# Earlier rows, an earlier tail for the next-to-last batch, and q stacked by PE for two batches

## What is computed

```python
x = x + jnp.tanh(g_xattn[0]) * _L0_xattn_ref(_layernorm(x, axis=-1), ctx_1024, ...)
x = x + jnp.tanh(g_ffn[0]) * _L0_ffn_ref(_layernorm(x, axis=-1), ...)
x = x + jnp.tanh(g_xattn[1]) * _L1_xattn_ref(_layernorm(x, axis=-1), ctx_1024, ctx_1024, mask, ...)
x = x + jnp.tanh(g_ffn[1]) * _L1_ffn_ref(_layernorm(x, axis=-1), ...)
```

## Time and profile before

| | |
|---|---|
| Three runs | 451.64, 458.64, 460.27 us |
| The profiled execution | 455.05 us, of which the span is 453.3 us |
| PE busy | 339.5 us (75% of the span) |
| PE weight loads | 249.3 us (55%) |
| DVE busy | 253.6 us (56%) |
| ACT busy | 156.5 us (35%) |
| POOL busy | 149.8 us (33%) |
| TensorE's granted clock, mean | 0.855 of 2.4 GHz |

### The profile page before, as it was taken

How to read it: one execution, slowest core, us unless ns; L and a number is a source line. 1 busy time by engine, 2 the same in 40 slices (tenths; PEclk the granted TensorE clock), 3 DMA queues, 4 the chain that set the end, 5 groups by cost and what they waited for, 6 DMA issues and landing times. The chain is left out here.

```text
span 453.3 us, 6857 instructions
## 1 busy us (share of the span) xinstructions
PE 339.5 (75%) x2066; PEld 249.3 (55%) x2066; DVE 253.6 (56%) x846; ACT 156.5 (35%) x370; POOL 149.8 (33%) x172
## 2 busy tenths in 40 slices
PE   2468979888969776466887999997577719988870
PEld 2236545545435665465664575653277609878770
DVE  2759565666365566136747677865463604535542
ACT  2312344434322253124222455362221305444440
POOL 3211211215040340431062102274536565645560
PEclk9867699998695899569869999999787867999995
DMA  7436987940044283776440231013565366869934
GB/s 268 128 75 158 300 230 220 290 133 17 2 148 136 78 246 101 242 219 164 106 129 6 62 80 48 14 35 91 196 199 168 119 172 191 284 187 324 371 139 139
DMA packets 67908, 70.42 MB, mean 155 GB/s; under 512 B 7933, under 2 KB 50691, under 8 KB 67872
## 3 DMA queue, kind: packets, MB, share of 16 engines
q1 hardware_dynamic: 41904, 52.24, 39.6%
q10 hardware_dynamic: 22448, 11.41, 8.7%
q0 software_dynamic: 3520, 6.34, 4.3%
HBM read 40.66 MB, written 21.81 MB: 138 GB/s over the span
## 5 line engine op out<-in xcount | busy, mean ns | idle before, releaser
L963 PE MATMUL ps_s<-xT,fw 128*128 128x128 f32 x488 | 77.7, 303 | 17.0 <-DVE xT L1301 8.6
L963 PEld LDWEIGHTS ps_s<-xT,fw 128*128 128x128 f32 x488 | 69.4, 215 | 20.1 <-DVE xT L1301 10.4
L668 ACT ACTIVATE probs<-ps_s 103x512 f32<-103x512 f32 (+1 forms) x96 | 56.2, 596 | 65.4 <-PE ps_s L872 57.8
L1152 DVE TENSOR_REDUCE negm<-ps_a 128x4 f32<-128x308 f32 x128 | 55.1, 470 | 29.5 <-PE ps_a L852 23.1
L574 POOL DMA_INDIRECT routed<-pay,slot x48 | 48.0, 1001 | 57.1 <-DVE slot L1261 45.9
L592 POOL DMA_INDIRECT expert_out<-xt x46 | 45.8, 996 | 35.1 <-ACT xt L733 25.2
L852 PE MATMUL ps_a<-ks,qs 128*128 128x308 f32 x128 | 42.3, 366 | 10.4 <-DVE negm L1152 5.5
L1291 DVE SCALAR_TENSOR_TENSOR qr<-qr,ps_s 128x256 f32<-128x256 f32 x46 | 19.2, 418 | 53.9 <-ACT qr L723 32.6
L871 PE MATMUL ps_s<-qs,ks 128*103 128x512 f32 (+1 forms) x96 | 47.7, 496 | 1.9 <-issue 0.7
L548 POOL TENSOR_SCALAR ve<-mv 128x4 f32<-128x4 f32 x16 | 3.7, 230 | 121.1 <-DVE mv L1102 121.1
L872 PE MATMUL ps_s<-augT,aug 128*103 128x512 f32 (+1 forms) x96 | 40.3, 420 | 0.0
(11 more groups left out here) (156 smaller groups left out, 559.6 us busy)
## 6 DMA issues: line engine op xcount, KB each, us to landing
fw<-f_in SPq DMA_DIRECT2D x46, 384.0 KB
routed<-xt ACTq DMA_DIRECT2D x2, 5568.0 KB, 23.8
fw<-f_in SPq DMA_DIRECT2D x30, 321.0 KB
qs<-qhl SPq DMA_DIRECT2D x128, 64.0 KB, 2.0
xt<-routed SPq DMA_DIRECT2D x46, 65.0 KB
xt<-routed SPq DMA_DIRECT2D x30, 64.0 KB
routed<-xt SPq DMA_DIRECT2D x30, 64.0 KB
routed<-pad SPq DMA_DIRECT2D x18, 65.0 KB, 2.1
```

Of the source, the lines that this page charges most:

```text
L668: nc.scalar.activation(probs[0:KSIZE[j], s, :], ps_s[(NS * n + s) % SCORE_BANKS][0:KSIZE[j], :], ACT.Exp, scale=SCALE).then_inc(exp_ok, 1)
L963: last = nc.tensor.matmul(up_bank[j % 2][:, c * P:(c + 1) * P], weights_of(j)[:, c * P:(c + 1) * P], xT[j % 2][:, :], start=True, stop=True)
L1152: nc.vector.tensor_reduce(negm[:, i, g * HPG:(g + 1) * HPG], a[:, 0:GK].rearrange("p (h k) -> p h k", h=HPG), AX.X, ALU.max, negate=True). ...
```

## The change

**An earlier tail for n = 2 and n = 6.** A new table moves their stages. In steps from the layer's first score tile: normalise2 47 to 44, turn2 47 to 45, router 49 to 46, route_exp 50 to 47, ranks 52 to 48, the four scatters 53, 55, 58, 59 to 49, 49, 50, 50. stats2 stays at 43.

**Earlier rows for parts 1 and 3.** The part's first three row loads are issued five steps before the part instead of all seven one step before; the rest follow one a step.

**An earlier second layer.** `SECOND` goes from 95 to 93, and with it all of that layer's steps. In `RETURNED_FRONT` the results of n = 6 stay at 99, and its high half moves into the step of its projection.

**q of n = 4 and 5 stacked by PE.** For these two batches the 16 DMAs are gone. PE multiplies each half by a selection matrix, two matmuls of 128x512 per group. Even groups go to ps_t and are copied out by ACT, odd groups to the ring and are copied out by DVE. The selection tile grows from 1024 to 1280 columns, so that one tile serves k and q.

```diff
+TAIL_NEXT_TO_LAST = {
+    "stats2": 19, "normalise2": 20, "turn2": 21, "router": 22, "route_exp": 23, "ranks": 24,
+    "scatter0": 25, "scatter1": 25, "scatter2": 26, "scatter3": 26,
+}
-SECOND = 95
+SECOND = 93
 RETURNED_FRONT = [
-    {"gather": 70, "results": 77, "stats": 77, "normalise": 78, "turn": 79, "project": 80, "high": 81, "low": 81, "maxima": 85,
-     "split": 93, "augment": 93},
-    {"gather": 73, "results": 82, "stats": 82, "normalise": 83, "turn": 85, "project": 87, "high": 88, "low": 88},
-    {"gather": 90, "results": 99, "stats": 99, "normalise": 100, "turn": 101, "project": 102, "high": 103, "low": 103},
-    {"gather": 93, "results": 104},
+    {"gather": 70, "results": 77, "stats": 77, "normalise": 78, "turn": 79, "project": 80, "high": 81, "low": 81, "spread": 82, "maxima": 83,
+     "split": 91, "augment": 91},
+    {"gather": 73, "results": 82, "stats": 82, "normalise": 83, "turn": 85, "project": 87, "high": 88, "low": 88, "spread": 90},
+    {"gather": 90, "results": 99, "stats": 99, "normalise": 100, "turn": 101, "project": 102, "high": 102, "low": 102},
+    {"gather": 93, "results": 103},
 ]
+BY_PE = [NB, NB + 1]
...
-                        if k == TILE_AT[p] + max(-1, t - ROWS_AHEAD):
+                        if k == TILE_AT[p] + max(-5 if p % 2 else -1, t - ROWS_AHEAD):
                             load_rows(p, t)
                 for n in due("low", k):
-                    spread_q(n)
+                    if n not in BY_PE:
+                        spread_q(n)
...
+            def take_even(n):
+                act.wait_ge(sc_full, NS * (n - 2))
+                for i, g in enumerate(range(0, GROUPS, 2)):
+                    act.wait_ge(q_turn, 2 * BY_PE.index(n) + i + 1)
+                    nc.scalar.activation(qs[n % 3][:, g, :], ps_t[:, :], ACT.Copy).then_inc(q_even, 1)
...
+            def spread_q(n):
+                pe.wait_ge(qh_ok, n + 1)
+                pe.wait_ge(ql_ok, n + 1)
+                for g in range(GROUPS):
+                    if g % 2 == 0:
+                        turn_bank_free(q_even, 2 * BY_PE.index(n) + g // 2 + 1)
+                    bank = ring() if g % 2 else ps_t
+                    for c in range(2):
+                        last = nc.tensor.matmul(bank[:, :], copies(Q_COPIES, c, g), qhl[c][n % 2][:, :], start=c == 0, stop=c == 1)
+                    last.then_inc(ring_full if g % 2 else q_turn, 1)
...
+            def take_odd(n):
+                dve.wait_ge(sc_full, NS * (n - 2))
+                for g in range(1, GROUPS, 2):
+                    a = ring()
+                    nc.vector.tensor_copy(qs[n % 3][:, g, :], a[:, :]).then_inc(q_odd, 1)
```

More of the change, by code:

```diff
@@ L131, in at_step, with spreads_by_pe @@
         return SECOND_FRONT + AT[stage]
-    return SECOND * l + NS * b + (TAIL[stage] if b == NB - 1 and stage in TAIL else AT[stage])
+    tail = {NB - 1: TAIL, NB - 2: TAIL_NEXT_TO_LAST}.get(b, {})
+    return SECOND * l + NS * b + tail.get(stage, AT[stage])
+def spreads_by_pe(k):
+    return [n for n in BY_PE if at_step(n, "spread") == k]
 def due(stage, k):
@@ L212, in two_layers @@
         cx4 = sb("cx4", [P, NB, HPG, KEYS])
-        select = sb("select", [P, 2, GROUPS, 4, 32], F32R)
+        select = sb("select", [P, GROUPS, 10, 32], F32R)
         maski = sb("maski", [P, TPB, KEYS], I32)
@@ L351, in pay_rows, with by_dma @@
             return slice((n % 2) * TPB, (n % 2 + 1) * TPB)
+        def by_dma(n):
+            return len([m for m in range(n % 3, n + 1, 3) if m not in BY_PE])
         def score_tile(s):
@@ L534, in link @@
                 pool.wait_ge(s_pool, chain.next() + 1)
[L536 removed]
+            nc.gpsimd.memset(select[:, :, :, :].bitcast(F32), 0.0).then_inc(s_select, 1)
             nc.gpsimd.memset(half[:, :], -0.5)
@@ L642, in _ @@
             act.wait_ge(ld_id, 16)
-            for c in range(2):
-                nc.scalar.activation(select[:, c, :, 2 * c:2 * c + 2, :], bcast(ident.rearrange("p (g r) -> p g r", g=GROUPS), 2, 2), ACT.Copy).then_inc(s_select, 1)
+            for pair in (select[:, :, 6:8, :], select[:, :, 1:4:2, :]):
+                nc.scalar.activation(pair, bcast(ident.rearrange("p (g r) -> p g r", g=GROUPS), 2, 2), ACT.Copy).then_inc(s_select, 1)
             def copy_nT(n):
@@ L651, in high_q @@
                 act.wait_ge(q_ok, n + 1)
-                if n >= 2:
+                if n - 2 in BY_PE:
+                    act.wait_ge(q_even, 2 * (BY_PE.index(n - 2) + 1))
+                    act.wait_ge(q_odd, 2 * (BY_PE.index(n - 2) + 1))
+                elif n >= 2:
                     for g in range(GROUPS):
-                        act.wait_ge(qspread[(n - 2) % 3][g], 64 * ((n - 2) // 3 + 1))
+                        act.wait_ge(qspread[(n - 2) % 3][g], 64 * by_dma(n - 2))
                 nc.scalar.activation(qhl[0][n % 2][:, :], qr1[:, :], ACT.Copy).then_inc(qh_ok, 1)
+            def take_even(n):
[3 more added lines that the diff above has]
+                    nc.scalar.activation(qs[n % 3][:, g, :], ps_t[:, :], ACT.Copy).then_inc(q_even, 1)
             def copy_augT(n):
@@ L755, in _ @@
                         nc.scalar.activation(aug[:, :, :].rearrange("p g k -> p (g k)"), augf, ACT.Copy).then_inc(s_aug, 1)
+                for n in spreads_by_pe(k):
+                    take_even(n)
                 for n in due("augment", k):
@@ L788, in ring, with copies @@
                 return ps_a[u % RING]
+            def copies(at, c, g):
+                return select[:, g, at[c]:at[c] + 4, :].rearrange("p b r -> p (b r)")
             def keys(l):
@@ L805, in spread_keys @@
                     for c in range(2):
-                        last = nc.tensor.matmul(bank, select[:, c, g, :, :].rearrange("p c r -> p (c r)"), khl[c][:, :], start=c == 0, stop=c == 1)
+                        last = nc.tensor.matmul(bank, copies(K_COPIES, c, g), khl[c][:, :], start=c == 0, stop=c == 1)
                     last.then_inc(ring_full if l else k_full, 1)
@@ L819, in values, with turn_bank_free @@
                 last.then_inc(ring_full, 1)
-            def transposes(src, done, read, value):
+            def turn_bank_free(read, value):
                 if reader:
@@ L824, in transposes @@
                 reader.append((read, value))
+            def transposes(src, done, read, value):
+                turn_bank_free(read, value)
                 for i in range(TPB):
@@ L844, in scores_for_max @@
                     pe.wait_ge(ks_ok, 2 * (l + 1))
-                if i == 0:
-                    pe.wait_ge(qspread[n % 3][g], 64 * (n // 3 + 1))
+                if i == 0 and n in BY_PE:
+                    pe.wait_ge((q_even, q_odd)[g % 2], 2 * BY_PE.index(n) + g // 2 + 1)
+                elif i == 0:
+                    pe.wait_ge(qspread[n % 3][g], 64 * by_dma(n))
                 bank = ring()
@@ L1147, in low_q @@
                 nc.vector.tensor_tensor(qhl[1][n % 2][:, :], qr1[:, :], qhl[0][n % 2][:, :].bitcast(F32), ALU.subtract).then_inc(ql_ok, 1)
+            def take_odd(n):
[3 more added lines that the diff above has]
+                    nc.vector.tensor_copy(qs[n % 3][:, g, :], a[:, :]).then_inc(q_odd, 1)
+                    dve.wait_ge(q_odd, 2 * BY_PE.index(n) + g // 2 + 1)
+                    dve.sem_inc(ring_used, 1)
             def maxima(n, u):
@@ L1337, in _ @@
                     low_q(n)
+                for n in spreads_by_pe(k):
+                    take_odd(n)
                 for n in due("output", k):
```

2 lines of the change are left out of this document (added).

## The result

The changed kernel takes 463.65 us (median of 4 runs, 463.13 to 468.62) where the kernel before took 455.82 (4 runs, 451.64 to 460.27): a ratio of 1.027, 95% interval 1.017 to 1.037. Two of the four runs of the kernel before, 458.64 and 460.27 us, lie over 1.5% above its fastest and are left out of the ratio, so it stands for 12 us, where the medians differ by 7.8. It is slower, and by more than was forecast: the sum was +9.4 on the profiled execution, and 465 us is 6.4 above the median of 458.64.

The account below looks back on a forecast made before the run. PE, busy 75% of the span, plus its waits was taken as the bound. Terms +7 - 3 + 1.4 + 0.5 + 6.5 - 1 - 2 = +9.4 on 455.05 gave 464.5; 465 us was predicted, range 446 to 472.

Parts of the forecast that it names:

- The first layer's end: End of the first layer's attention: PE's work moved behind pay's wait runs at half clock, ranks waits for choose; +7 us.
- Part 1's rows: Step from part 0 to part 1: PE's idle 7.13 us shrinks, gather starts later, results of n = 4 come sooner; -3 us.
- The front: Second layer's front, 211.00 to 229.80: two steps fewer against q's DVE copies and PE matmuls; +1.4 us, bounds -4 and +5.
- The two steps: Before the second layer's first score tile: two steps fewer, half of 3.2 us taken as gain; -1.6, bounds 0 and -3.2.
- nothing covers the matmuls: Upper bound for the second layer's front, +5 us: q's matmuls on PE find no empty time to cover them.
- n = 6: High half in its projection's step: ACT may wait for DVE's bias, with tiles queued behind it; +0.5 us.
- The second layer's end: PE's 3.03 us move behind pay's wait, ranks waits for choose, part 2's rows' wait is filled; +6.5 us, bounds +5.1 and +8.0.
- Parts 2 and 3: Part 3's row wait of 1.19 us goes, -1 us; scatters of n = 6 issued ahead of part 2's put-outs, -2 us.
- POOL's relief: Part 2: n = 6's eight scatters precede the put-outs, two of them leaving the back-to-back run; -2 us, bounds 0 and -15.
- D: Rival, chance 0.15: SP's row loads delay the last write-back and gather by 4.5 us, n = 4's results follow; 472 us.
- C: Rival, chance 0.18: released clock, and the late waits in 347.50 to 374.40 go, -12 instead of -2; 443.6 us.
- B: Rival, chance 0.22: moved matmuls release the throttled clock, so both layers' ends cost less; about 454 us.

## Why the prediction was right, and where its steps were not

The forecast was 465 us in a range of 446 to 472; 463.65 was measured. That it came so close is in good part luck. The forecast stood on runs of 451.64 to 460.27 us, and the kernel before, run beside the experiments, takes about 452: the change costs 12 us by the ratio and 13.5 in the trace, where +9.4 was summed. And of the seven terms four come out near in this trace, two are too small and one is too large; one of the four, the rows, does so in this trace only.

- **The first layer's end.** Forecast +7, bounds +1.7 and +7.7 (its terms add up to 5.5 + 1.9 = 7.4 at most); the trace has +4.3, the tail of n = 2 alone costs 1.009. The mechanism is as told, with a wait of 6.60 us where some 6.5 was written. The moved work and the wait of ranks came as priced: 5.1 us, where 5.5 was written, and 1.33. What was mis-sized is what followed at half clock before: the router is 0.9 us shorter, weigh2 0.4, and the copies of k and the turns behind it 1.2. The granted clock was 0.50 from 133.37 to 138.5, then full until about 142, 0.50 again through most of weigh2, and full from about 145.6; the kernel before stayed at 0.50 from 135.05 to 146.96. The rule of the Trainium skill, page "TensorE: Matmul & The Clock Gate", section "What's actually happening", by which activity releases the throttle, is borne out here more than the row of before made me grant. It did not hold for long: after ranks' wait of 1.33 us, five small matmuls and the first of two of 308 columns, the half clock was back. At the second layer's end of the changed kernel the router did not get the full clock (1.71 us); with the tail alone it did (1.01).
- **Part 1's rows.** Forecast -3, built of 5 us on PE and a gather 4.5 us later. The trace: -6.0, then +2.9, together -3.1. But the three other traces with the same edit have -0.9, -1.1 and -1.9 over these two stretches, and those without it +0.1 to -2.1, so a gain of 3 us is not there, and the rows alone are worth nothing (1.001). The step that failed is that the results would come with the gather and so 3 us sooner: they do wait for the gather now, and it comes too late to gain. The last write-back is 5.4 us later and the first gather 6.0, of which 2.6 are the first layer's end; from part 0's first tile on they come 2.7 and 3.3 us later, where 4.5 was written.
- **The front.** Forecast +1.4; the trace has +5.4. The two steps show -1.2 alone (forecast -1.6), which is inside the scatter. The step that failed priced q by its copies on DVE, 3.0 us, and let PE's empty 5.2 us cover the matmuls. They don't cover: each of the two trains stands bare on PE for 2.5 us, with DVE waiting for it and copying, 4.4 us in the trace with q alone. The bound of +5 for "nothing covers the matmuls" was the case. The two parts make 3.2 of the 5.4 us; the rest is not assigned.
- **n = 6.** Forecast +0.5 for its halves in one step; the trace has +5.2, and moving its front two steps back is worth 1.2% of the kernel. This is the largest miss. The diff leaves its results at step 99 while the first score tile moves to 93, so they begin six tiles in and not four. I had read this only for the halves. weigh0 stands five steps behind the first tile, so it now precedes the results, where before it lay between results and turn and filled 1.9 us (240.37 to 242.22): the wait for the rows grows from 2.63 to 4.82 us, and what follows runs at half clock. q comes 1.83 us too late for the max pass; in two other traces with the same table it is 0.46 and 0.30.
- **The second layer's end.** Forecast +6.5; the trace has +7.3, and +6.5 with the tail alone. It holds, with 5.51 us of wait, ranks waiting 2.18, and the wait of 1.62 us for part 2's rows gone.
- **Parts 2 and 3.** Forecast -3 together; the trace has -3.9. The wait of 1.19 us for part 3's rows is gone, as forecast. POOL's relief was named but undersized for the tail by itself, -5.9: I counted two scatters in the run of 354 to 371 and overlooked the six that stood among part 2's first put-outs.
- **The rivals.** D, the binding gather, is refuted in its size: the results of n = 4 begin 4.2 us after the fourth gather's issue, not 10.6. Its mechanism is there, since DVE now waits 5.05 us for that gather. C did not come: ACT's unascribed waits are still 6.07 and 4.60 us. One of before's three is gone and the others are shorter, which the prediction had named as a sign of being wrong. SP's freed queue did not do it, since the changed kernel with the old tail still has three (3.74, 6.58 and 5.25). The tail alone has two (6.02 and 4.57), but so has q by PE alone (5.88 and 5.97), so their number decides little. B's clock came in part.

Not settled: what ACT, DVE and PE wait for in the unascribed waits. Shown is only that they stand beside runs of indirect DMAs on POOL, that in the one trace with a shortened run there are none beside part 1's gathers, and that moving SP's pads away does not remove them.

## What to carry to other kernels

When a table shifts a whole block, list the stages whose absolute step stays: each of them has moved too, relative to its cover, and one such entry (n = 6's results) cost as much as both tails. A transfer that is off the path should not be replaced by work on engines that are on it: 2.5 us of PE per batch cost 0.6% for both batches and 1.0% for one, where PE never waited for SP's 10.3 us of transfers in the kernel before. An earlier router moved ahead of PE's other work costs what it uncovers; what it can give back here came with its DMAs being out before the next stage wanted POOL's queue. Moving the scatters alone, without PE, gained 0.7%, though not in the stretch where the gain was expected. And when a forecast is an absolute time, the few runs that it starts from are one of its terms.

## What the hardware did that I had not expected

Beside indirect DMAs back to back on POOL, engines that do not use them waited for causes that the profile does not name. Eight gathers in a row beside part 1 went with a wait of 5.81 us on DVE and 3.70 on ACT, and four in a row with none. A run of eight is not enough by itself: the gathers of n = 6 and 7 in the kernel before, from 227.41 to 237.3 us, have no such wait beside them, and the same eight in two other kernels have one on ACT (5.34 and 4.47 us). SP's own issues took longer beside such runs: the eight pad rows of part 3 took 8.36 us to issue in the changed kernel beside n = 7's scatters (7.1 in the kernel before), and those of part 2, with no indirect DMA beside them, 3.85:

```profile
319.52 3.85 SPq L457 DMA_DIRECT2D routed<-pad  x8
...
369.99 8.36 SPq L457 DMA_DIRECT2D routed<-pad  x8
```
